# A pipelined cross-attention: the maximum of a slot spread over the partitions by DMA instead of TensorE and ScalarE

## The chip, the cores and the metric

The program runs on one core of one Trainium2 chip. The metric is the device time of one execution in microseconds (us): lower is better. An execution is timed from launch to end; the profile of one execution shows the engines of that core from their first to their last instruction. Engine names: PE is TensorE (PEld its weight loads), DVE is VectorE, ACT is ScalarE, POOL is GpSimd, SP is SyncE, which here only issues DMAs.

## What is computed

The reference is one layer of a perceiver: cross-attention of 8 batches of 128 latents to 2048 context rows each, then differential self-attention, then a mixture of 8 experts, each added to the input. Only the cross-attention is touched here:

```python
q = (query @ wq.T + bq)   # 8 batches x 128 rows, 16 heads of 32
k = (key @ wk.T + bk)     # 8 batches x 2048 rows
v = (value @ wv.T + bv)
scores = einsum('bhqd,bhkd->bhqk', q, k) / sqrt(32)
attn = softmax(scores, axis=-1)
ctx = einsum('bhqk,bhkd->bhqd', attn, v)
return ctx @ wo.T + bo
```

## The kernel before

Five stages follow each other: queries and the first context chunk (names with a_), the cross-attention (b_), its output projection (c_), the projections of the self-attention (d_), and the self-attention with the experts (e_ and f_). The change lies in the second, the function cross_attention.

A slot is one batch and one group of four heads (HG = 4), so there are 32 slots (SLOTS). A slot takes four chunks (CHUNK) of 512 context rows. Scores are computed with context rows on the partitions and the 4 x 128 queries of four heads along the free axis. A softmax over context rows then runs partly across partitions. For the maximum the kernel first reduces elementwise over all 16 blocks of a slot, into b_mx (128 partitions x 4 heads x 128 queries). TensorE transposes b_mx into a bank (the unit "M"), DVE reduces each row to one number per query and head (b_top, 128 x 4), and now queries lie on partitions. These 512 numbers have to come back as one row that all 128 partitions hold (b_mb, 128 x 512), since the subtraction `b_s - b_mb` (L892) has context rows on the partitions again. Before the change this way back is: ACT copies b_top 128 times wide into b_spread (L849), TensorE transposes b_spread (the unit "B", four transposes at L765), ACT copies the bank into b_mb (L837).

All engines follow one clock of "beats", eight to a slot, written out by hand: at each beat every engine's program runs the steps whose rule names that beat. The functions `score_step`, `exp_step`, `turned_slot` and so on hold the rules. For slot m, counted from its own beats:

- beat 8m+27: TensorE runs M(m). Beat 8m+28: DVE reduces it to b_top, and before, ACT spreads it and TensorE ends the beat with B(m). Beat 8m+29: ACT moves B(m) to b_mb.
- even beats: TensorE computes the scores of one chunk into the four banks b_psS (L720, 16 matmuls); DVE takes them into b_mx in four steps (L926, L929); in the next, odd beat ACT moves all of b_psS to one of seven buffers b_s (L871), and only then may TensorE write the next chunk's scores there.
- even beats, five chunks behind the scores: DVE subtracts the maximum (L892), ACT takes the exponential (L854), POOL adds the four blocks up for the denominators (L650 for a slot's first chunk, twice L655 for each other one). The first chunk of slot m has its turn at beat 8m+30.
- beats 2 mod 4: TensorE multiplies two chunks of exponentials with the values (L734). Beat 8m+40: it sums the denominators (L757), DVE takes the reciprocal and normalizes (L914, L918), ACT adds a bias (L861).
- every beat up to 255: TensorE projects one unit of keys or values, 12 matmuls of 128x512 (L43 to L45), into one of three banks b_work, which M and B share too; ACT takes each away in the next beat (L809, L821 or L830). DVE transposes a block of the context (L882), ACT rounds it (L846), POOL takes the rest (L639), SP loads the block after next (L222, four DMAs).

TAIL is 28: the last four slots sum their denominators on TensorE (L748) in place of POOL. From beat 256 on nothing is projected any more. Within an engine everything runs in the order of its program; between engines semaphores order it.

Of the kernel before, what the change touches and what calls it, by code (L numbers as in the profile page):

```python
# [7 lines left out]
F32 = mybir.dt.float32  # L8
F32R = mybir.dt.float32r
BF16 = mybir.dt.bfloat16  # L10
ALU = mybir.AluOpType
# [4 lines left out]
P = 128  # L16
# [432 lines left out]
def cross_attention(nc, x, ctx_in, w, q_d, o_d, cin, kT, shared):  # L449

    with ExitStack() as ctx:
# [74 lines left out]
        for beat in range(FIRST, LAST):  # L526
            if (x0 := projected(beat)) is not None:
                p0, u0 = x0
                enter(("KV"[u0 // CHUNK], p0, u0 % CHUNK), beat)
            if (s0 := turned_slot(beat)) is not None:  # L530
                enter(("M", s0, 0), beat)
            if (s0 := spread_slot(beat)) is not None:
                enter(("B", s0, 0), beat)

        def value_places(b, t):
# [22 lines left out]
        psO = ctx.enter_context(nc.psum_tensor("b_psO", [P, 512], F32))  # L558

        const = sem("b_const")  # L560
        turned = sem("b_turned")
        bias_in = sem("b_bias_in")
        q_in = [sem(f"b_q_in{i}") for i in range(3)]
# [20 lines left out]
        def _(sp):  # L584
# [12 lines left out]
            sp.wait_ge(turned, 1)  # L597
            load_blocks(sp, ctx_in, cin, shared.raw_in, 2, 2)
            for beat in range(FIRST, LAST):
                if (x0 := turned_next(beat - 1)) is not None and x0[0] * CHUNK + x0[1] + 2 < SLOTS * CHUNK:  # L600
                    u = x0[0] * CHUNK + x0[1]
                    sp.wait_ge(turned, u - 2 * CHUNK + 1)
                    load_blocks(sp, ctx_in, cin, shared.raw_in, *divmod(u + 2, CHUNK))
                n = score_step(beat - 1)
                if n is not None and n % CHUNK == CHUNK - 1 and n // CHUNK + 3 < SLOTS:

                    sp.wait_ge(s_full, n + 1)
                    load_queries(n // CHUNK + 3)
                n = normal_slot(beat - 1)
                if n is not None and n < SLOTS - 1:  # L610
                    b, g = divmod(n, G)
                    sp.wait_ge(o_done, n + 1)
                    sp.dma_start(o_d[g, b, :, :], o_st[:, n % 2, :]).then_inc(o_out[n % 2], 16)
                if beat == SLOTS * SLOT + 2:

                    sp.wait_ge(work_full, RING["V", SLOTS - 1, CHUNK - 1] + 1)
                    sp.dma_start(shared.wo, w["wo"].rearrange("(o p) d -> p o d", p=P)).then_inc(shared.wo_in, 16)
                    sp.dma_start(shared.x1, x.rearrange("b p d -> p b d")).then_inc(shared.x_in, 16)
                if n == SLOTS - 3:

                    for i in range(2):
                        sp.wait_ge(o_out[i], 16 * G * (B - 1) // 2)
                    for g in range(G):
                        sp.dma_start(shared.o_sb[:, g, 0:B - 1, :], o_d[g, 0:B - 1].rearrange("b p t -> p b t")
                                     ).then_inc(shared.o_in[0], 16)
                if n == SLOTS - 2:
                    for i in range(2):
                        sp.wait_ge(o_out[i], 16 * (SLOTS // 2 - i))
                    for g in range(G - 1):
                        sp.dma_start(shared.o_sb[:, g, B - 1, :], o_d[g, B - 1]).then_inc(shared.o_in[1], 16)  # L630
# [39 lines left out]
        def _(pe):  # L670
            pe.wait_ge(const, 1)

            def wait_evicted(unit):
                if unit is not None:
                    kind, m, n = unit
                    if kind == "K":
                        pe.wait_ge(k_done, m * CHUNK + n + 1)
                    elif kind == "V":
                        pe.wait_ge(v_done, m * CHUNK + n + 1)
                    elif kind == "M":  # L680
                        pe.wait_ge(top_done, m + 1)
                    else:
                        pe.wait_ge(mb_done, m + 1)

            def bank_of(unit):
                wait_evicted(LAST_IN[unit])
# [81 lines left out]
            for beat in range(FIRST, LAST):  # L768
# [11 lines left out]
                        values(p, u - CHUNK)  # L780
                if (m := turned_slot(beat)) is not None:
                    turn("M", m, mx, mx_done, (m + 1) * MAXIMA)
                if (m := spread_slot(beat)) is not None:
                    turn("B", m, spread, spread_done, m + 1)
                    if m == SLOTS - 1:

                        pe.wait_ge(shared.wo_in, 16)
# [1 line left out]
                        for k in range(KD):  # L789
# [2 lines left out]
                                                           shared.wo[:, o, k * P:(k + 1) * P], ident[:, :])  # L792
                            last.then_inc(shared.wo_full, 1)

        @block.scalar
        def _(act):
            act.wait_ge(bias_in, 32)
            for beat in range(FIRST, LAST):
                if beat > FIRST and (x0 := projected(beat - 1)) is not None:
# [11 lines left out]
                    else:  # L811
# [11 lines left out]
                        else:  # L823
# [4 lines left out]
                            else:  # L828
                                out = rows[:, :, at[0]:at[0] + P]
                            nc.scalar.activation(out, bank[:, :].rearrange("p (g r) -> p g r", g=G),  # L830
                                                 ACT.Copy).then_inc(v_done, 1)
                if (m := spread_slot(beat - 1)) is not None:
                    i, bank = RING["B", m, 0], work[BANK["B", m, 0]]
                    act.wait_ge(work_full, i + 1)

# [6 lines left out]
                if (x0 := transposed(beat)) is not None:  # L842
# [1 line left out]

                    act.wait_ge(turned, (p - 2) * CHUNK + k + 1)
                    nc.scalar.activation(cT[0][:, p % 2, k, :], cin[:, 1, k % 2, :], ACT.Copy).then_inc(hi_done, 1)  # L846
                if (m := spread_slot(beat)) is not None:
                    act.wait_ge(top_done, m + 1)
                    nc.scalar.activation(spread[:, :, :], top[:, m % 2, :].rearrange("p (j o) -> p j o", o=1)  # L849
                                         .broadcast_to([P, HG, P]), ACT.Copy).then_inc(spread_done, 1)  # L850
                if (n := exp_step(beat)) is not None:
                    act.wait_ge(sub_done, n + 1)
                    part = s[:, n % BUFS, :, :].rearrange("p t n -> p (t n)")
                    nc.scalar.activation(part, part, ACT.Exp, scale=SCALE).then_inc(exp_done, 1)  # L854
                if (m := normal_slot(beat)) is not None:
                    g = m % G
                    act.wait_ge(od_free, m + 1)
# [5 lines left out]
                if (n := move_step(beat)) is not None:  # L863

                    act.wait_ge(mx_done, CHUNK * (n + 1))
                    if n >= BUFS:

                        act.wait_ge(pv_done, n - BUFS + 1)
                        if (n - BUFS) // CHUNK < TAIL:
                            act.wait_ge(sum_done, sums_of(n - BUFS))  # L870
                    nc.scalar.activation(s[:, n % BUFS, :, :].rearrange("p t (j q) -> p t j q", j=HG),  # L871
                                         psS[:, :, :].rearrange("p j (t q) -> p t j q", t=CHUNK),
                                         ACT.Copy).then_inc(s_moved, 1)

        @block.vector
        def _(dve):
            def context_turned(p, k):

                u = (p - 2) * CHUNK + k
# [4 lines left out]
            dve.wait_ge(bias_in, 32)  # L884
            context_turned(2, 0)
            for beat in range(FIRST, LAST):
                if (n := exp_step(beat)) is not None:
                    m, c = divmod(n, CHUNK)
                    dve.wait_ge(s_moved, n + 1)
                    if c == 0:  # L890
                        dve.wait_ge(mb_done, m + 1)
                    nc.vector.tensor_tensor(  # L892
                        s[:, n % BUFS, :, :], s[:, n % BUFS, :, :],
                        mb[:, :].rearrange("p (o n) -> p o n", o=1).broadcast_to([P, CHUNK, HG * P]),
                        ALU.subtract).then_inc(sub_done, 1)
                if (m := spread_slot(beat)) is not None:
                    i, bank = RING["M", m, 0], work[BANK["M", m, 0]]
                    dve.wait_ge(work_full, i + 1)

                    reached(dve, spread_done, m - 1)  # L900
                    nc.vector.tensor_reduce(top[:, m % 2, :], bank[:, :].rearrange("p (j k) -> p j k", j=HG),
                                            AX.X, ALU.max).then_inc(top_done, 1)
                if (m := normal_slot(beat)) is not None:
# [17 lines left out]
                if (n := score_step(beat)) is not None:  # L921
                    dve.wait_ge(s_full, n + 1)
                    for t in range(CHUNK):
# [3 lines left out]
                        else:  # L927
                            dve.wait_ge(mx_done, n * CHUNK + t)
                            nc.vector.tensor_tensor(mx[:, :, :], part, mx[:, :, :], ALU.max).then_inc(mx_done, 1)  # L929


def transpose_units(nc, pe, bank, ident, src, blocks, u, full, lo_done):
# [1038 lines left out]
```

## Time and profile before

| | us |
|---|---|
| median of 3 runs | 1692.62 |
| lowest and highest of them | 1683.69 and 1693.33 |
| the profiled execution | 1690.8 |
| its span, first to last instruction | 1689.0 |

The mean granted clock of TensorE in the profiled execution is 0.973 of full speed. The span is 1.8 us shorter than the execution's own time. The cross-attention lies between about 71 and 1130 us of the span.

### The profile page before, as it was taken

To read this page: it belongs to the slowest core of one execution; us is meant where nothing else is said; L and a number is where in the kernel's file an instruction comes from. 1 tells how busy PE (TensorE), PEld (TensorE's weight loads), DVE (VectorE), ACT (ScalarE), POOL (GpSimd) and SP (SyncE) were. 2 spreads that over 40 slices of the span, in tenths; PEclk is the share of its full clock that TensorE was granted. 3 is DMA by queue.
4 is the path that set the end of the run, shared out by engine and by line. 5 is a ranking of instruction groups with operands and counts; after the bars stand their busy time and mean duration, and the time that the engine had idled before them with its cause. 6 is when DMAs were issued, how large, how long until landed. Compare 5 with 4: busy or idle time off the path is not lost. (4 is left out here: it accounts for less than half of the span.)

```text
span 1689.0 us, 36984 instructions
## 1 busy us (share of the span) xinstructions
PE 1619.8 (96%) x15589; PEld 1314.5 (78%) x15604; DVE 1179.0 (70%) x1523; ACT 950.8 (56%) x1437; POOL 899.7 (53%) x472
## 2 busy tenths in 40 slices
PE   7999999999999999999999999667998899999999
PEld 6788888888888888888888887556886677777787
DVE  5137888888888888888888887877434577653322
ACT  4347776777767777777777776662103677630000
POOL 0026788888878878888887885002000344522220
PEclk9999999999999999999999999788999799899999
DMA  5332222222222222222222210213422111211001
GB/s 187 75 50 35 36 39 40 39 38 37 38 37 42 36 36 40 41 36 37 37 40 37 40 24 5 80 53 113 165 88 94 38 51 51 65 50 50 28 23 50
DMA packets 310404, 88.75 MB, mean 53 GB/s; under 512 B 259392, under 2 KB 292160, under 8 KB 310240
## 3 DMA queue, kind: packets, MB, share of 16 engines
q1 hardware_dynamic: 310240, 86.39, 22.2%
q8 instruction: 124, 2.03, 0.5%
q14 instruction: 40, 0.33, 0.1%
HBM read 71.67 MB, written 14.68 MB: 51 GB/s over the span
## 5 line engine op out<-in xcount | busy, mean ns | idle before, releaser
L655 POOL TENSOR_TENSOR b_acc<-b_acc,b_s 128x1024 f32<-128x1024 f32 x168 | 563.6, 3355 | 12.4 <-ACT b_s L854 5.3
L892 DVE TENSOR_TENSOR b_s<-b_s,b_mb 128x2048 f32<-128x2048 f32 x128 | 398.0, 3111 | 28.4 <-ACT b_mb L837 28.4
L929 DVE TENSOR_TENSOR b_mx<-b_psS,b_mx 128x512 f32<-128x512 f32 x480 | 330.8, 689 | 93.3 <-PE b_psS L720 80.2
L854 ACT ACTIVATE b_s<-b_s 128x2048 f32<-128x2048 f32 x128 | 244.3, 1909 | 18.3 <-DVE b_s L892 15.2
L871 ACT ACTIVATE b_s<-b_psS 128x2048 f32<-128x2048 f32 x128 | 241.2, 1885 | 20.9 <-DVE b_mx L929 20.9
L43 PE MATMUL b_work<-wvT,cT 128*128 128x512 f32 x496 | 202.9, 409 | 0.0
L43 PE MATMUL b_work<-cT,wkT 128*128 128x512 f32 x496 | 200.3, 404 | 1.7 <-POOL b_ones L636 1.7
L44 PE MATMUL b_work<-wvT,cT 128*128 128x512 f32 x496 | 194.5, 392 | 0.0
L44 PE MATMUL b_work<-cT,wkT 128*128 128x512 f32 x496 | 194.2, 392 | 0.0
L45 PE MATMUL b_work<-wvT,cT 128*128 128x512 f32 x496 | 193.8, 391 | 0.0
L45 PE MATMUL b_work<-cT,wkT 128*128 128x512 f32 x496 | 193.4, 390 | 0.0
L639 POOL TENSOR_TENSOR cT<-cin,cT 128x512 fp32r<-128x512 f32 x120 | 156.1, 1301 | 54.8 <-ACT cT L846 54.8
L720 PE MATMUL b_psS<-b_q,b_kT 32*128 32x128 f32 x4096 | 153.8, 287 | 12.9 <-ACT b_s L871 12.8
L809 ACT ACTIVATE b_kT<-b_work,b_bk 128x512 f32<-128x512 f32 x124 | 85.5, 689 | 140.5 <-PE b_work L45 140.5
L720 PEld LDWEIGHTS b_psS<-b_q,b_kT 32*128 32x128 f32 x4096 | 129.3, 190 | 38.7 <-issue 38.7
L650 POOL TENSOR_TENSOR b_acc<-b_s 128x1024 f32<-128x1024 f32 x28 | 68.8, 2456 | 129.7 <-PE b_psO L757 127.8
L734 PE MATMUL b_psO<-b_s,v_sb 128*32 128x128 f32 x4096 | 129.7, 278 | 2.5 <-issue 1.8
L734 PEld LDWEIGHTS b_psO<-b_s,v_sb 128*32 128x32 f32 x4096 | 110.3, 111 | 24.8 <-issue 24.4
L43 PEld LDWEIGHTS b_work<-cT,wkT 128*128 128x128 f32 x496 | 93.0, 187 | 27.5 <-POOL b_ones L636 2.1
L882 DVE STREAM_TRANSPOSE cin<-cin 128x512 f32<-128x512 f32 x120 | 83.8, 699 | 41.7 <-DMA b_bv<-in_L_xattn_bv 19.5
L43 PEld LDWEIGHTS b_work<-wvT,cT 128*128 128x128 f32 x496 | 93.1, 188 | 24.6
L1707 ACT ACTIVATE e_sm<-e_psS,e_low 128x128 f32<-128x128 f32 x256 | 90.1, 383 | 37.7 <-DVE e_low L1782 37.7
(290 smaller groups left out, 2802.4 us busy)
## 6 DMA issues: line engine op xcount, KB each, us to landing
cin<-in_ctx SPq DMA_DIRECT2D x480, 64.0 KB, 2.4
experts_sb<-in_L_ffn_expert_w SPq DMA_DIRECT2D x8, 1024.0 KB, 5.3
q_scratch<-d_st SPq DMA_DIRECT2D x16, 256.0 KB, 2.3
k_scratch<-d_st SPq DMA_DIRECT2D x16, 256.0 KB, 2.3
e_q<-q_scratch SPq DMA_DIRECT2D x16, 256.0 KB, 2.7
k_sb<-k_scratch SPq DMA_DIRECT2D x16, 256.0 KB, 2.9
cin<-in_ctx SPq DMA_DIRECT2D x4, 512.0 KB, 8.4
b_kT<-in_x SPq DMA_DIRECT2D x4, 512.0 KB, 8.0
```

The lines of the kernel that those rows point to most:

```text
L43: nc.tensor.matmul(out, lhs[0], rhs[0], start=first, stop=False)
L44: nc.tensor.matmul(out, lhs[0], rhs[1], start=False, stop=False)
L45: return nc.tensor.matmul(out, lhs[1], rhs[0], start=False, stop=last)
L639: nc.gpsimd.tensor_tensor(cT[1][:, p % 2, k, :], cin[:, 1, k % 2, :], f32(cT[0][:, p % 2, k, :]), ALU.subtract).then_inc(split_done, 1)
L655: nc.gpsimd.tensor_tensor(acc[:, :, :], acc[:, :, :], s[:, buf, 2 * i:2 * i + 2, :], ALU.add).then_inc(sum_done, 1)
L720: last = nc.tensor.matmul(psS[:, j, t * P:(t + 1) * P], kT[h, at + t * P:at + (t + 1) * P], q[h, m % 3, :], start=True, stop=True)
L734: last = nc.tensor.matmul(psO[j * HD:(j + 1) * HD, 0:P], v[:, at + j * HD:at + (j + 1) * HD], s[:, n % BUFS, i, j * P:(j + 1) * P], start= ...
L854: nc.scalar.activation(part, part, ACT.Exp, scale=SCALE).then_inc(exp_done, 1)
L871: nc.scalar.activation(s[:, n % BUFS, :, :].rearrange("p t (j q) -> p t j q", j=HG), psS[:, :, :].rearrange("p j (t q) -> p t j q", t=CHUN ...
L892: nc.vector.tensor_tensor(s[:, n % BUFS, :, :], s[:, n % BUFS, :, :], mb[:, :].rearrange("p (o n) -> p o n", o=1).broadcast_to([P, CHUNK, ...
L929: nc.vector.tensor_tensor(mx[:, :, :], part, mx[:, :, :], ALU.max).then_inc(mx_done, 1)
L1707: last = nc.scalar.activation(sm[:, hf, i, j % 2, u, :], psS[:, j, u, :], ACT.Exp, bias=low[:, hf, j, u:u + 1], scale=-1.0, accum_out=sums ...
```

## The change

For slots 0 to 27 the way back from b_top to b_mb goes through DRAM. SP waits for b_top, stores its 512 numbers to a scratch tensor (one element of four bytes each, so that four rows of 128 queries lie one behind the other), waits until they have landed, and loads that row of 2 KB into all 128 partitions of b_mb. This stands in SP's program at beat 8m+29, ahead of the loads of the context block. The unit B, ACT's spread and ACT's move are gone for these slots; slots 28 to 31 keep them.

For the same slots the first chunk's subtraction moves on DVE from the start of its beat (8m+30) to the end, behind the maxima of that beat, and ACT's exponential of it from beat 8m+30 to the end of beat 8m+31, behind that beat's move of b_psS. The other three chunks of a slot keep their places.

```diff
-            if (s0 := spread_slot(beat)) is not None:
+            if (s0 := spread_slot(beat)) is not None and s0 >= TAIL:
                 enter(("B", s0, 0), beat)
...
+        top_d = nc.dram_tensor("top_scratch", [TAIL, HG, P], F32).ap()
+        top_out = [sem(f"b_top_out{i}") for i in range(2)]
+        mb_in = sem("b_mb_in")
...
             for beat in range(FIRST, LAST):
+                if (m := spread_slot(beat - 1)) is not None and m < TAIL:
+                    sp.wait_ge(top_done, m + 1)
+                    with nc.allow_non_contiguous_dma(reason="512 numbers"):
+                        sp.dma_start(top_d[m].rearrange("j p -> p j"), top[:, m % 2, :]).then_inc(top_out[m % 2], 16)
+                    sp.wait_ge(top_out[m % 2], 16 * (m // 2 + 1))
+
+                    reached(sp, sub_done, m * CHUNK)
+                    sp.dma_start(mb[:, :], top_d[m].rearrange("(o j) p -> o (j p)", o=1).broadcast_to([P, HG * P])
+                                 ).then_inc(mb_in, 16)
...
-                if (m := spread_slot(beat)) is not None:
-                    turn("B", m, spread, spread_done, m + 1)
+                if (m := spread_slot(beat)) is not None and m >= TAIL:
+                    turn("B", m, spread, spread_done, m - TAIL + 1)
...
+        def late(n):
+
+            return n % CHUNK == 0 and n // CHUNK < TAIL
...
-                if (m := spread_slot(beat - 1)) is not None:
+                if (m := spread_slot(beat - 1)) is not None and m >= TAIL:
...
-                if (m := spread_slot(beat)) is not None:
+                if (m := spread_slot(beat)) is not None and m >= TAIL:
                     act.wait_ge(top_done, m + 1)
...
-                if (n := exp_step(beat)) is not None:
-                    act.wait_ge(sub_done, n + 1)
...
+                if (n := exp_step(beat)) is not None and not late(n):
+                    exponentials(n)
...
+                if (n := exp_step(beat - 1)) is not None and late(n):
+                    exponentials(n)
...
+            def less_maximum(n):
+                m, c = divmod(n, CHUNK)
+                dve.wait_ge(s_moved, n + 1)
+                if c == 0 and m < TAIL:
+                    dve.wait_ge(mb_in, 16 * (m + 1))
+                elif c == 0:
+                    dve.wait_ge(mb_done, m - TAIL + 1)
...
-                if (n := exp_step(beat)) is not None:
-                    m, c = divmod(n, CHUNK)
...
+                if (n := exp_step(beat)) is not None and not late(n):
+                    less_maximum(n)
...
-                    reached(dve, spread_done, m - 1)
+                    if m >= TAIL + 2:
+                        dve.wait_ge(spread_done, m - TAIL - 1)
+                    elif m >= 2:
+                        dve.wait_ge(top_out[m % 2], 16 * (m // 2))
...
+                if (n := exp_step(beat)) is not None and late(n):
+                    less_maximum(n)
```

On PE, at the seam between the value units of beats 8m+28 and 8m+29, the program before reads:

```order
L43 MATMUL b_work<-wvT_69,cT_52 128x512
L44 MATMUL b_work<-wvT_70,cT_52 128x512
L45 MATMUL b_work<-wvT_69,cT_53 128x512
L765 MATMUL b_work<-ident,b_spread 128x128 x4
L43 MATMUL b_work<-wvT_69,cT_52 128x512
L44 MATMUL b_work<-wvT_70,cT_52 128x512
```

The four transposes of b_spread stand between two units of the projection; in the changed program the units follow each other there, and nothing else on PE moves.

On DVE, from the subtraction of a slot's last chunk to that of the next slot's second one, the program before (L892 is the subtraction, L901 the reduction to b_top, L882 the context's transpose, L926 and L929 the maxima, L914 and L918 the normalization):

```order
L892 TENSOR_TENSOR b_s<-b_s,b_mb 128x2048
L901 TENSOR_REDUCE b_top<-b_work 128x4
L882 STREAM_TRANSPOSE cin<-cin 128x512
L926 COPY b_mx<-b_psS 128x512
L929 TENSOR_TENSOR b_mx<-b_psS,b_mx 128x512 x3
L892 TENSOR_TENSOR b_s<-b_s,b_mb 128x2048
L882 STREAM_TRANSPOSE cin<-cin 128x512
L929 TENSOR_TENSOR b_mx<-b_psS,b_mx 128x512 x4
L892 TENSOR_TENSOR b_s<-b_s,b_mb 128x2048
L914 RECIPROCAL b_rD<-b_psO 128x128
L918 TENSOR_TENSOR b_oq<-b_psO,b_rD 128x128
```

And the changed program at the same place (L906 is the subtraction, L931 the reduction, L916 the transpose, L956 and L959 the maxima):

```order
L906 TENSOR_TENSOR b_s<-b_s,b_mb 128x2048
L931 TENSOR_REDUCE b_top<-b_work 128x4
L916 STREAM_TRANSPOSE cin<-cin 128x512
L956 COPY b_mx<-b_psS 128x512
L959 TENSOR_TENSOR b_mx<-b_psS,b_mx 128x512 x3
L916 STREAM_TRANSPOSE cin<-cin 128x512
L959 TENSOR_TENSOR b_mx<-b_psS,b_mx 128x512 x4
L906 TENSOR_TENSOR b_s<-b_s,b_mb 128x2048 x2
L944 RECIPROCAL b_rD<-b_psO 128x128
L948 TENSOR_TENSOR b_oq<-b_psO,b_rD 128x128
```

The first chunk's subtraction went past one transpose and one set of maxima, so that it stands directly ahead of the second chunk's.

## Rows read from the trace of the kernel before

**Rows 1.** The page, part 1: busy time and share of the engines.

```profile
PE 1619.8 (96%) x15589; PEld 1314.5 (78%) x15604; DVE 1179.0 (70%) x1523; ACT 950.8 (56%) x1437; POOL 899.7 (53%) x472
```

**Rows 2.** The view by stretches: one slot; PE, PEld, DVE, ACT, POOL busy, clock, DMA.

```profile
615.00:647.40 32.40, 32.40 (x377) 26.26 (x376) 27.86 (x28) 23.27 (x23) 27.47 (x12) 1.00 0.23 38
```

**Rows 3.** The waits of PE, whole run: total us, times, longest.

```profile
PE b_psS L720 <- ACT b_s L871: 12.8, 6, 5.0
...
PE b_work L765 <- DVE b_mx L929: 9.2, 3, 3.1
```

**Rows 4.** Timeline of PE in that slot: start, us, line, operation, out<-in.

```profile
619.24 0.39 PE L45 MATMUL b_work<-wvT,cT 128*128 128x512 f32 x1
619.47 0.60 PE L765 MATMUL b_work<-ident,b_spread 128*128 128x128 f32 x4
619.83 0.48 PE L43 MATMUL b_work<-wvT,cT 128*128 128x512 f32 x1
620.14 0.39 PE L44 MATMUL b_work<-wvT,cT 128*128 128x512 f32 x1
...
624.64 1.17 PE L720 MATMUL b_psS<-b_q,b_kT 32*128 32x128 f32 x32
...
631.45 0.64 PE L757 MATMUL b_psO<-b_acc,b_ones 128*32 128x128 f32 x16
...
638.79 1.96 PE L734 MATMUL b_psO<-b_s,v_sb 128*32 128x128 f32 x64
640.67 1.17 PE L720 MATMUL b_psS<-b_q,b_kT 32*128 32x128 f32 x32
```

**Rows 5.** Timeline of DVE: the first slot's second subtraction, then that slot.

```profile
142.89 2.28 DVE L892 TENSOR_TENSOR b_s<-b_s,b_mb 128x2048 f32<-128x2048 f32 x1
...
615.97 0.68 DVE L901 TENSOR_REDUCE b_top<-b_work 128x4 f32<-128x512 f32 x1
...
620.86 3.21 DVE L892 TENSOR_TENSOR b_s<-b_s,b_mb 128x2048 f32<-128x2048 f32 x1 [0.84 <-ACT b_mb L837]
...
625.88 2.87 DVE L929 TENSOR_TENSOR b_mx<-b_psS,b_mx 128x512 f32<-128x512 f32 x4 [1.19 <-PE b_psS L720]
628.66 2.28 DVE L892 TENSOR_TENSOR b_s<-b_s,b_mb 128x2048 f32<-128x2048 f32 x1
632.16 0.96 DVE L914 RECIPROCAL b_rD<-b_psO 128x128 f32<-128x128 f32 x1 [1.22 <-PE b_psO L757]
...
633.98 2.83 DVE L929 TENSOR_TENSOR b_mx<-b_psS,b_mx 128x512 f32<-128x512 f32 x4
636.73 3.70 DVE L892 TENSOR_TENSOR b_s<-b_s,b_mb 128x2048 f32<-128x2048 f32 x1
```

**Rows 6.** Timeline of ACT in that slot.

```profile
631.55 0.60 ACT L830 ACTIVATE v_sb<-b_work 128x512 f32<-128x512 f32 x1 [0.34 <-PE b_work L45]
632.05 0.62 ACT L846 ACTIVATE cT<-cin 128x512 fp32r<-128x512 f32 x1
632.57 1.91 ACT L854 ACTIVATE b_s<-b_s 128x2048 f32<-128x2048 f32 x1
...
636.85 1.89 ACT L871 ACTIVATE b_s<-b_psS 128x2048 f32<-128x2048 f32 x1
```

**Rows 7.** Timeline of POOL: its first accumulation, then that slot.

```profile
143.40 4.02 POOL L650 TENSOR_TENSOR b_acc<-b_s 128x1024 f32<-128x1024 f32 x1 [1.94 <-ACT b_s L854]
...
619.51 6.81 POOL L655 TENSOR_TENSOR b_acc<-b_acc,b_s 128x1024 f32<-128x1024 f32 x2
626.27 1.30 POOL L639 TENSOR_TENSOR cT<-cin,cT 128x512 fp32r<-128x512 f32 x1
632.27 2.39 POOL L650 TENSOR_TENSOR b_acc<-b_s 128x1024 f32<-128x1024 f32 x1 [4.70 <-PE b_psO L757]
```

**Rows 8.** POOL's L655 alone: durations of one, ns, least/median/most.

```profile
L655 POOL TENSOR_TENSOR b_acc<-b_acc,b_s x168: 2393/2435/4341, 148.7 to 1043.5; 128x1024 f32<-128x1024 f32 x168
```

**Rows 9.** DMA issues by tensor: KB each, median us from issue to landing.

```profile
cin<-in_ctx SPq DMA_DIRECT2D x480, 64.0 KB, 2.4
...
c_bo<-in_L_xattn_bo SPq DMA_DIRECT2D x1, 256.0 KB, 3.2
...
b_bk<-in_L_xattn_bk SPq DMA_DIRECT2D x1, 2.0 KB, 2.5
```

More of the change, by code:

```diff
@@ L682, in wait_evicted @@
                     else:
-                        pe.wait_ge(mb_done, m + 1)
+                        pe.wait_ge(mb_done, m - TAIL + 1)
             def bank_of(unit):
@@ L793, in _, with exponentials @@
                             last.then_inc(shared.wo_full, 1)
+        def late(n):
+            return n % CHUNK == 0 and n // CHUNK < TAIL
         @block.scalar
         def _(act):
+            def exponentials(n):
+                act.wait_ge(sub_done, n + 1)
+                part = s[:, n % BUFS, :, :].rearrange("p t n -> p (t n)")
+                nc.scalar.activation(part, part, ACT.Exp, scale=SCALE).then_inc(exp_done, 1)
             act.wait_ge(bias_in, 32)
@@ L850, in _ @@
                                          .broadcast_to([P, HG, P]), ACT.Copy).then_inc(spread_done, 1)
-                if (n := exp_step(beat)) is not None:
-                    act.wait_ge(sub_done, n + 1)
-                    part = s[:, n % BUFS, :, :].rearrange("p t n -> p (t n)")
-                    nc.scalar.activation(part, part, ACT.Exp, scale=SCALE).then_inc(exp_done, 1)
+                if (n := exp_step(beat)) is not None and not late(n):
+                    exponentials(n)
                 if (m := normal_slot(beat)) is not None:
@@ L873, in _ @@
                                          ACT.Copy).then_inc(s_moved, 1)
+                if (n := exp_step(beat - 1)) is not None and late(n):
+                    exponentials(n)
         @block.vector
         def _(dve):
+            def less_maximum(n):
[5 more added lines that the diff above has]
+                    dve.wait_ge(mb_done, m - TAIL + 1)
+                nc.vector.tensor_tensor(
+                    s[:, n % BUFS, :, :], s[:, n % BUFS, :, :],
+                    mb[:, :].rearrange("p (o n) -> p o n", o=1).broadcast_to([P, CHUNK, HG * P]),
+                    ALU.subtract).then_inc(sub_done, 1)
             def context_turned(p, k):
@@ L886, in _ @@
             for beat in range(FIRST, LAST):
-                if (n := exp_step(beat)) is not None:
-                    m, c = divmod(n, CHUNK)
[L889 to L895, printed above, removed]
+                if (n := exp_step(beat)) is not None and not late(n):
+                    less_maximum(n)
                 if (m := spread_slot(beat)) is not None:
```

## The prediction

> **What bounds the kernel now.** I read the busy shares first: PE is at 96% of the span, DVE at 70%, the others lower [rows 1]. That is an average, so the second view is the one by stretches, cut to one slot of the cross-attention: in 32.40 us PE is busy for 32.40, at a granted clock of 1.00, the upper of its two levels (2.4 GHz); DVE is busy 27.86, POOL 27.47, ACT 23.27 [rows 2]. PE has no gap at all there, so a slot is worth what PE's instructions take, and only what leaves PE's queue can shorten it. The third view, PE's waits over the whole run, says the same from the other side: the waits in this stage are few, 12.8 us in 6 for the scores' banks and 9.2 us in 3 for the maxima [rows 3]. They lie almost wholly in the last four slots, where nothing is projected any more and which the change leaves alone. The fourth view is the timeline of the engines in that same slot, where I look for what PE comes close to waiting for. I keep the trace's own times below and move PE's marks behind B by what B's removal gives.
>
> **What is removed.** Per slot four transposes leave PE. Their busy time of 0.60 us overlaps their neighbours, so I go by starts. The last matmul of one unit starts at 619.24 and the transposes at 619.47, a step of 0.23. The next unit starts at 619.83, and its second matmul at 620.14 [rows 4]. Without the transposes the next unit would start at 619.47 and its second matmul 0.23 later, at 619.70. The gain is 620.14 - 619.70 = 0.44 us a slot, and 28 x 0.44 = 12.3 us in all. The bounds of this term from the same rows: 0.36 (619.83 - 619.47, if the slow first step comes back elsewhere) gives 10.1, the full 0.60 gives 16.8. I take 0.44 because it counts to where the steady step has returned.
>
> ACT loses its spread and its move to b_mb, both off the path: it was idle 9 us of the slot [rows 2], so they are worth nothing. DVE's wait of 0.84 us for b_mb [rows 5] goes too, and buys nothing either, since DVE next waits 1.19 us for the scores.
>
> **What is added, first the two DMAs.** The trace has no store of 512 single numbers. The nearest rows: the load of a bias of 512 numbers with the same strides, landed 2.5 us after its issue, and the context loads, landed after 2.4. The load of one 2 KB row into 128 partitions exists, as c_bo: 3.2 us [rows 9]. b_top is ready at 615.97 + 0.68 = 616.65 [rows 5], so b_mb is ready at about 616.65 + 2.5 + 3.2 = 622.4. The subtraction that needs it comes at 628.2 (below): 5.8 us to spare. The lower bound of the chain is 2.4 + 2.4, the upper one I set by letting the store take three times its row: 7.5 + 3.2, at 627.4, still in time. So the term is 0 at either end. SP's queue: the block's four loads stand behind the pair and go out about 6 us later. They land in 2.4 us and are used two transposes later, some 16 us on, so this is hidden too. DMA engines were busy 0.23 of the slot [rows 2].
>
> The Trainium skill, "DMA: Bandwidth & Descriptors", Specifications, speaks against this store: below 512 bytes a descriptor is a read-modify-write. It gives no price for 512 of them. The trace here shows loads of such pieces only; no row shows the store, and by the margin above the rule would have to cost more than 5 us to matter.
>
> **What is moved, and what comes close.** The first chunk's subtraction now follows the maxima of its beat. In the new schedule PE's marks behind B are 0.44 earlier: the scores at 624.20, the denominators at 631.01, the values' product at 638.35, the next scores but one at 640.23 [rows 4]. That last one must find b_psS moved by ACT. This is the wait I check.
>
> How long a subtraction takes depends on POOL. It took 2.28 at 628.66, while POOL stood idle between 627.57 and 632.27, but 3.21 at 620.86 and 3.70 at 636.73 with POOL at work [rows 5, 7]. The pair of L655 beside the one at 620.86 took 6.81, where one alone takes about 2.4 [rows 7, 8]: 619.51 + 2.4 = 621.9, then the subtraction until 624.07, then the second accumulation until 626.3. And the first L650 of the kernel, started at 143.40 inside the subtraction of 142.89 to 145.17, took 4.02 in place of 2.4, ending 2.3 us after it. One simply waits for the other. The Trainium skill, "SBUF — State Buffer", Who interferes with whom, states this as an exclusive lock held for a whole instruction; by that rule, the trace agrees. Had I gone by the rows' mere durations instead, the moved subtraction would keep 3.21 and the margin below would be nearly gone.
>
> Now DVE, step by step. Maxima of the beat: start 625.88 - 0.44 = 625.44, end 2.78 later (628.66 - 625.88), 628.22. POOL's accumulations of the slot before ended at 626.27 with one subtraction inside; that subtraction has moved away, so POOL is through earlier, about 625, and its rest step L639 too. It is idle then, because L650 needs the exponential. So: first subtraction 628.22 to 630.50, second to 632.78, both at 2.28. Then reciprocal, normalization and transpose, 633.98 - 632.16 = 1.82, to 634.60 (the denominators are there since 631.7). Then the next maxima, 636.73 - 633.98 = 2.75, to 637.35, which is 0.62 later than before. ACT's move follows, 1.89, to 639.3 [rows 6]. PE wants to start the scores at 640.23: 0.9 us to spare, no wait.
>
> ACT: the move of the beat's scores ends at about 630.8 (628.22, a take-away of 0.6, 1.9), the late exponential at 632.7, take-away and rounding 0.60 + 0.62, the second exponential at 635.8 [rows 6]. The product of values needs it at 638.35: 2.5 to spare. POOL starts L650 at 632.7 in place of 632.27 and has the earlier 2.3 us in hand. DVE's fourth subtraction ends at about the time it did, so M and the reduction stay in place.
>
> **The sum.** 12.3 us gained on PE, nothing given back. From the profiled execution: 1690.8 - 12.3 = 1678.5. That execution lies 1.8 below the median of the three runs shown, which run from 1683.69 to 1693.33.
>
> **Rivals.**
> - *Late maxima (slower).* The place is the scores at 640.23 behind ACT's move. It decides once DVE is more than 0.9 us later than I have it. This would be so if the two subtractions don't get 2.28 each. For it: they now stand back to back, DVE works through what it had spread out, and two more durations exist in the rows. Against it: POOL has nothing to do just then. At 3.21 each the delay is 1.86, the wait 1.0 with a signal between engines, the net loss 1.0 - 0.44 = 0.5 to 0.6 a slot: +16, 1707. At 3.70 each the delay is 2.84, the net loss about 1.5: +42, 1733. The trace of the first is nearer.
> - *No gain.* Half of that delay, 1.3 us a slot, costs just the 0.44: 1690.8. Or the step over the seam comes back at another instruction. For it: another queue (the scores' banks) is within 0.9 us of PE. Against: PE waited there for nothing in the slot.
> - *The DMA chain is late.* It decides above 11.6 us (628.22 - 616.65) for store and load, twice the rows' sum. At 14 us the first subtraction would be 2.4 late, the wait on PE 1.5, the net 1.1 a slot: +30, 1721. No row speaks for a landing that long at a DMA share of 0.23.
> - *It doesn't do what it says.* PE's program has 5252 rows against 5280, so 28 units are gone, one a slot. I give this nothing.
>
> **How the numbers follow.** Forecast 0.74, late maxima 0.12, no gain 0.10, late DMA 0.04. About 1% is what a measurement of this kernel can tell from no change (the three runs spread over 0.6%). The forecast is a gain of 0.73% and falls within it; the spread of the runs and the upper bound of the PE term (16.8) put 0.14 beyond 1%. Late maxima at 1707 is still just within 1%, the heavier form and the late DMA are not: 0.09 slower. The rest, 0.77, is the same. The range takes the PE term's bounds (1674 to 1680.7), 3 us for the runs' spread below, and reaches up past the case of no gain: 1671 to 1694. What is left out is the late maxima and the late DMA, 0.16.
>
> **What would show it.** Right: a slot of 31.96 us with PE busy throughout; B's transposes 16 in place of 128; the first and second subtraction about 2.28 each, back to back; the first not preceded by a wait for a DMA; ACT's move ending about 0.9 us ahead of the scores; the store landing in about 2.5 us and b_mb in 3.2. Wrong: rows of PE at the scores waiting for ACT's b_s inside slots 0 to 27, subtractions of 3 us or more there, or DVE waiting for b_mb<-top_scratch.

## The result, and the profile after

The change makes the kernel slower: 1739.26 us (median of 4 runs, 1729.22 to 1744.48) against 1688.15 for the kernel before, a ratio of 1.030 with a 95% interval of 1.023 to 1.036. The profiled execution took 1744.48, with a span of 1742.7. Executions of one and the same kernel here fall on two levels some 8 us apart (before: 1683.7 and 1692.6), and the difference lies in the stages behind the cross-attention, so I compare stretches inside the stage where I can.

The busy shares, to be laid beside [rows 1]:

```profile
PE 1627.5 (93%) x15477; PEld 1319.1 (76%) x15492; DVE 1115.6 (64%) x1523; ACT 912.6 (52%) x1381; POOL 850.4 (49%) x472
```

PE lost its 112 transposes (15589 to 15477 instructions) and is nevertheless busy for longer, 1627.5 us against 1619.8, while its share falls. The first suggests that it ran at a lower clock somewhere, the second that it waits. PE's waits in the run after, against [rows 3] (12.8 in 6 there):

```profile
PE b_psS L733 <- ACT b_s L891: 48.5, 31, 5.0
...
PE b_psS L733 <- issue: 8.6, 8, 3.9
```

So 25 more waits at the scores for ACT's move, nearly one a slot, and eight in which PE waited for nothing that the profile names. Now one slot, in order. SP's timeline with the two new DMAs:

```profile
371.07 0.39 SPq L607 DMA_DIRECT2D top_scratch<-b_top  x1
379.91 0.33 SPq L611 DMA_DIRECT2D b_mb<-top_scratch  x1
```

DVE in the same slot (its counterpart is [rows 5]):

```profile
370.35 0.69 DVE L931 TENSOR_REDUCE b_top<-b_work 128x4 f32<-128x512 f32 x1 [0.24 <-PE b_work L778]
...
385.42 4.49 DVE L906 TENSOR_TENSOR b_s<-b_s,b_mb 128x2048 f32<-128x2048 f32 x2 [2.42 <-DMA b_mb<-top_scratch]
389.83 0.95 DVE L944 RECIPROCAL b_rD<-b_psO 128x128 f32<-128x128 f32 x1
...
391.65 2.83 DVE L959 TENSOR_TENSOR b_mx<-b_psS,b_mx 128x512 f32<-128x512 f32 x4
```

And what PE meets at the scores, between two M units:

```profile
369.71 0.60 PE L778 MATMUL b_work<-ident,b_mx 128*128 128x128 f32 x4
...
396.54 1.17 PE L733 MATMUL b_psS<-b_q,b_kT 32*128 32x128 f32 x32 [1.54 <-ACT b_s L891]
...
403.22 0.60 PE L778 MATMUL b_work<-ident,b_mx 128*128 128x128 f32 x4
```

b_top is ready at 371.04 and SP issues the store at once, but can issue the load only at 379.91: the store takes 8.8 us, where I had put 2.5. The subtraction starts 5.5 after the load's issue, once the load has landed: DVE, idle for 2.42 until then, starts it 14.4 us after b_top. The pair of subtractions takes 4.49, as forecast. All that follows is late by the rest: maxima, ACT's move, and PE's scores by 1.54. The slot takes 403.22 - 369.71 = 33.51 us against 32.40 before [rows 2].

In the issue list the load has a median landing of 5.3 us, where c_bo had 3.2 [rows 9]:

```profile
b_mb<-top_scratch SPq DMA_DIRECT2D x28, 256.0 KB, 5.3
```

The distance from store to load on SP is 8.7 to 9.5 us in 20 of the 28 slots, and 9.7 to 11.4 in the others, seven of which stand in a row. In that row lies the worst of the "issue" waits. PE's timeline there:

```profile
622.49 0.73 PE L733 MATMUL b_psS<-b_q,b_kT 32*128 32x128 f32 x16
627.15 1.28 PE L733 MATMUL b_psS<-b_q,b_kT 32*128 32x128 f32 x16 [3.94 <-issue]
...
629.38 0.63 PE L45 MATMUL b_work<-wvT,cT 128*128 128x512 f32 x1
629.80 0.63 PE L43 MATMUL b_work<-wvT,cT 128*128 128x512 f32 x1
```

PE stops in the midst of one set of scores, whose data are all there, while the store of 615.60 is in flight (the load goes out at 627.01). PE goes on 0.14 us later. The end of the pause and the end of the store fall together in the other slots too: seven of the eight "issue" waits end within 0.6 us of the issue of the load, 8.8 to 11.6 us after the store's own. Afterwards PE's matmuls step by 0.42 to 0.43 us in place of 0.23 [rows 4]. The view by stretches (columns as in [rows 2]) shows the granted clock around it:

```profile
615.00:622.00 7.00, 7.00 (x77) 5.76 (x80) 4.46 (x7) 5.40 (x5) 6.92 (x4) 1.00 0.07 3
622.00:627.00 5.00, 1.22 (x38) 1.10 (x29) 0.00 (x0) 0.00 (x0) 2.55 (x2) 0.84 0.00 0
627.00:633.00 6.00, 5.85 (x28) 4.67 (x28) 4.43 (x5) 0.00 (x0) 0.00 (x0) 0.56 0.63 124
```

After the idle 4 us the clock is at its lower level of 1.2 GHz for some 5 us (0.56 of full over the third stretch, whose last piece has PE back at a step of 0.23). The DMA engines' share is 0.00 from 622 to 627, though the store isn't through.

### The profile page after: what moved, and what is told of

Read it like the earlier page. It is cut to its first block and busy times, and to the rows that moved or that the text cites. A ratio compares the mean times of both kernels' runs of the same rounds, so it can differ in the third digit from the quotient of the medians.

```text
span 1742.7 us, 36732 instructions
## 1 busy us (share of the span) xinstructions
PE 1627.5 (93%) x15477; PEld 1319.1 (76%) x15492; DVE 1115.6 (64%) x1523; ACT 912.6 (52%) x1381; POOL 850.4 (49%) x472
## 3 DMA queue, kind: packets, MB, share of 16 engines
q8 instruction: 123, 2.02, 0.6%
## 5 line engine op out<-in xcount | busy, mean ns | idle before, releaser
L668 POOL TENSOR_TENSOR b_acc<-b_acc,b_s 128x1024 f32<-128x1024 f32 x168 | 515.3, 3067 | 7.8 <-ACT b_s L817 0.9
L959 DVE TENSOR_TENSOR b_mx<-b_psS,b_mx 128x512 f32<-128x512 f32 x480 | 329.8, 687 | 155.1 <-PE b_psS L733 142.0
L906 DVE TENSOR_TENSOR b_s<-b_s,b_mb 128x2048 f32<-128x2048 f32 x128 | 333.0, 2621 | 61.7 <-DMA b_mb<-top_scratch 55.0
L733 PE MATMUL b_psS<-b_q,b_kT 32*128 32x128 f32 x4096 | 163.7, 292 | 57.3 <-ACT b_s L891 48.5
L733 PEld LDWEIGHTS b_psS<-b_q,b_kT 32*128 32x128 f32 x4096 | 136.9, 193 | 86.1 <-issue 85.8
L916 DVE STREAM_TRANSPOSE cin<-cin 128x512 f32<-128x512 f32 x120 | 84.3, 703 | 80.1 <-POOL cT L652 54.9
L852 ACT ACTIVATE v_sb<-b_work 128x512 f32<-128x512 f32 x80 | 47.5, 594 | 146.4 <-PE b_work L45 146.4
```

The source lines that it names most:

```text
L668: nc.gpsimd.tensor_tensor(acc[:, :, :], acc[:, :, :], s[:, buf, 2 * i:2 * i + 2, :], ALU.add).then_inc(sum_done, 1)
L733: last = nc.tensor.matmul(psS[:, j, t * P:(t + 1) * P], kT[h, at + t * P:at + (t + 1) * P], q[h, m % 3, :], start=True, stop=True)
L906: nc.vector.tensor_tensor(s[:, n % BUFS, :, :], s[:, n % BUFS, :, :], mb[:, :].rearrange("p (o n) -> p o n", o=1).broadcast_to([P, CHUNK, ...
```

## The experiments

Three theories stood at the start. Theory 1: b_mb comes too late, the rest is as forecast. Theory 2: the transfers disturb PE and its clock, whatever they bring. Theory 3: the late order of subtraction and exponential costs by itself. Softmax doesn't change when the same number is subtracted for one query and head throughout, so runs that subtract something else do the same work. Each run's diff is shown against the changed kernel where nothing else is said, and only its telling lines.

**No DMA of the maximum**

```diff
-                if (m := spread_slot(beat - 1)) is not None and m < TAIL:
-                    sp.wait_ge(top_done, m + 1)
...
+            nc.gpsimd.memset(mb[:, :], 1.0).then_inc(const, 1)
```

> The changed kernel without both DMAs: b_mb is set once to 1.0 by POOL, so that for slots 0 to 27 a constant is subtracted in place of the maximum; the order stays late, the unit B stays away. Theory 1 (the maximum comes too late, and everything else is as forecast): b_mb is always there, so PE gains its 0.44 us a slot and waits for nothing: 12 us less than before, about 1676 against 1688. Theory 2 (the two transfers disturb PE and its clock, whatever they bring): the same 1676. Theory 3 (the late order itself squeezes DVE and ACT so that PE waits at the scores): still about 1730 to 1740, with PE waiting 1 to 2 us a slot for ACT's move.

Measured: 1679.13, ratio 0.9926 (0.991 to 0.9943). Two M units of it, and DVE between them:

```profile
607.87 0.60 PE L770 MATMUL b_work<-ident,b_mx 128*128 128x128 f32 x4
...
639.82 0.60 PE L770 MATMUL b_work<-ident,b_mx 128*128 128x128 f32 x4
```

```profile
621.09 4.48 DVE L898 TENSOR_TENSOR b_s<-b_s,b_mb 128x2048 f32<-128x2048 f32 x2
```

The slot takes 31.95 us; 31.96 was forecast. The gain on PE and the back-to-back subtractions at 2.28 each are there. Theory 3 falls.

**The load alone**

```diff
-                        sp.dma_start(top_d[m].rearrange("j p -> p j"), top[:, m % 2, :]).then_inc(top_out[m % 2], 16)
-                    sp.wait_ge(top_out[m % 2], 16 * (m // 2 + 1))
...
-                    sp.dma_start(mb[:, :], top_d[m].rearrange("(o j) p -> o (j p)", o=1).broadcast_to([P, HG * P])
+                    sp.dma_start(mb[:, :], w["bk"].rearrange("(o n) -> o n", o=1).broadcast_to([P, HG * P])
```

> The changed kernel with the load but without the store: SP waits for b_top and loads 512 numbers of a bias into all partitions of b_mb, so a bias is subtracted in place of the maximum. Theory 1: the load alone lands 3 to 6 us after b_top, before the 11.6 us at which it is wanted: about 1676. Theory 2, if the load of 256 KB is what disturbs: 1690 to 1720, with waits of PE put down to issue. Theory 3: 1730 to 1740.

Measured: 1678.99, ratio 0.9922 (0.9905 to 0.9938). The load lands in 3.3 us and costs nothing. What is wrong lies in the store.

**The late order alone, in the kernel before** (the diff is against that kernel)

```diff
-                if (n := exp_step(beat)) is not None:
+                if (n := exp_step(beat)) is not None and not late(n):
...
+                if (n := exp_step(beat)) is not None and late(n):
+                    less_maximum(n)
```

> The kernel before with the late order alone: first chunk's subtraction and exponential moved as in the change, the unit B and ACT's copies kept, no DMA of the maximum. Theories 1 and 2: no difference from before beyond 0.3%, about 1688, PE 100% busy in a slot. Theory 3: slower by 40 us or more.

Measured: 1692.63, ratio 1.0009 (0.9994 to 1.0024), PE busy for 850.00 us of the 850 from 200 to 1050. The order is free.

**The store aside, and nobody waits**

```diff
+                    sp.dma_start(mb[:, :], w["bk"].rearrange("(o n) -> o n", o=1).broadcast_to([P, HG * P])
+                                 ).then_inc(mb_in, 16)
                         sp.dma_start(top_d[m].rearrange("j p -> p j"), top[:, m % 2, :]).then_inc(top_out[m % 2], 16)
-                    sp.wait_ge(top_out[m % 2], 16 * (m // 2 + 1))
```

> The same load from the bias, and behind it the store of b_top as in the changed kernel, for which nobody waits but the reduction two slots later; a bias is subtracted in place of the maximum. The store runs, but nothing hangs on it. Theory 1: about 1676, the store costs nothing. Theory 2: the store of 512 single numbers itself disturbs (instruction fetch of PE, context loads behind it): 1690 to 1720, with waits of PE put down to issue and a lower clock behind them. Theory 3: 1730 to 1740.

Measured: 1712.42, ratio 1.0117 (1.0086 to 1.0147), 33 us above the load alone. PE's waits:

```profile
PE b_psS L731 <- ACT b_s L889: 16.9, 14, 5.0
PE b_psS L731 <- issue: 15.9, 13, 2.6
```

b_mb is in time here, and few waits for ACT's move are added (16.9 us against 12.8 before); the waits put down to "issue" are the largest new group. From 200 to 1050 us there are 15 of them, and each ends 9.0 to 11.5 us after a store was issued. The store disturbs by itself, as theory 2 has it, in this form: four context loads stand right behind it in the queue.

**The same, but SP waits for the store before it goes on** (the diff is against the run above)

```diff
                         sp.dma_start(top_d[m].rearrange("j p -> p j"), top[:, m % 2, :]).then_inc(top_out[m % 2], 16)
+                    sp.wait_ge(top_out[m % 2], 16 * (m // 2 + 1))
```

> As the run with the store aside (b_mb from a bias, loaded first), but SP waits for the store before it goes on, so that its duration can be read; store and destination as in the change, 512 pieces of four bytes, neighbours next to each other in DRAM. A bias is subtracted in place of the maximum. The store takes 9 us or more between its issue and the next block load; the kernel is at 1700 to 1715 as with the store aside (1712), if the store's disturbance has to do with the store alone; at 1679, if it was the context loads queued behind it that disturbed.

Measured: 1681.65, ratio 0.9919 (0.9887 to 0.9952). From the store's issue to the next load it is 7.3 to 9.5 us. PE's waits for "issue" are down to:

```profile
PE b_psS L732 <- issue: 2.0, 4, 0.6
```

One wait of SP makes 31 us. The store alone in flight costs some 3 us by the medians (1681.65 against 1678.99, within the spread of its four runs, 1671.17 to 1686.41); it is costly with other loads queued behind it. These four waits too end within 0.4 us of the next load's issue, which is when SP has seen the store through. In the changed kernel SP waits as well, yet its profiled execution has eight of the "issue" waits. So this disturbance isn't tied to the loads queued behind alone.

**As late, without a store.** The first try:

```diff
+                    for i in range(5):
+                        sp.dma_start(spread[0:1, 0, :], w["bk"][0:P].rearrange("(o n) -> o n", o=1)).then_inc(idle_in, 16)
+                        sp.wait_ge(idle_in, 16 * (5 * m + i + 1))
```

> The changed kernel without the store, but as late: in its place SP loads 128 numbers of a bias five times, each waited for (about 2.1 us each), and then the bias into b_mb, so b_mb lands some 14 us after b_top as in the changed kernel; a bias is subtracted in place of the maximum. Theory 1 (lateness alone costs a wait of 1 to 2 us at the scores a slot, on top of what the store disturbs): 1700 to 1715 and PE's waits at the scores for ACT's move in nearly every slot. Theory 2 (it is all the store's disturbance): 1679.

Measured: 1678.96, ratio 0.9933 (0.9911 to 0.9954). It doesn't put theory 1 to the test: five loads took 6 us, so b_mb was there 9.7 us after b_top. It does bear out that 9.7 is early enough. With nine of them:

> As the run with five small loads in place of the store, but with nine, since five took only 6 us together and b_mb landed 9.7 us after b_top, still in time. Nine take about 10.9 us, and with the load's 3.6 b_mb lands 14.5 us after b_top, as in the changed kernel (9.0 + 5.3), 2.9 after the 11.6 at which DVE wants it. A bias is subtracted in place of the maximum. Theory 1 (lateness costs by itself): DVE waits 2 to 3 us for b_mb in each slot, PE 1 to 2 us at the scores for ACT's move, 1700 to 1720. Theory 2 (only the store's disturbance costs): 1679.

Measured: 1723.56 (four runs, 1715.83 to 1731.08), ratio 1.0172 (1.0148 to 1.0197), 45 us above the run with five. Waits of PE, and the slot's rows on DVE and PE:

```profile
PE b_psS L733 <- ACT b_s L891: 55.1, 33, 5.0
```

```profile
607.07 0.69 DVE L929 TENSOR_REDUCE b_top<-b_work 128x4 f32<-128x512 f32 x1 [1.89 <-PE b_work L778]
...
622.25 4.50 DVE L906 TENSOR_TENSOR b_s<-b_s,b_mb 128x2048 f32<-128x2048 f32 x2 [2.52 <-ACT b_s L891]
```

```profile
606.43 0.60 PE L778 MATMUL b_work<-ident,b_mx 128*128 128x128 f32 x4
...
633.36 1.17 PE L733 MATMUL b_psS<-b_q,b_kT 32*128 32x128 f32 x32 [1.64 <-ACT b_s L891]
...
640.09 0.60 PE L778 MATMUL b_work<-ident,b_mx 128*128 128x128 f32 x4
```

The subtraction starts 2.5 us after the maxima ended. The view puts this down to ACT, whose move of a later chunk ended just then, at 622.19; but the chunk subtracted here was moved five chunks earlier, and the load was issued at 618.74, with a median landing of 3.4 us in this run. It is the load. PE waits 1.64, the slot takes 33.66. Over the whole run PE's waits for ACT's move are 42 us more than in the kernel before (55.1 against 12.8 [rows 3]), and it has none of the "issue" waits at the scores. Without any store, lateness gives about three quarters of what separates the changed kernel from the load alone (45 of 1739.26 - 1678.99 = 60).

**What makes the store slow.** Four forms. First, 16 bytes a partition, heads innermost:

```diff
-                        sp.dma_start(top_d[m].rearrange("j p -> p j"), top[:, m % 2, :]).then_inc(top_out[m % 2], 16)
+                    sp.dma_start(top_d[m], top[:, m % 2, :]).then_inc(top_out[m % 2], 16)
...
+                    less = mb[:, :].rearrange("p (o q j) -> p o j q", o=1, j=HG).broadcast_to([P, CHUNK, HG, P])
```

> The changed kernel with the store as 128 pieces of 16 bytes (b_top as it lies, queries outermost) in place of 512 of four; the row loaded back then has the four heads innermost, and the subtraction reads b_mb with a step of four elements. Everything is computed. Theory A (the store's time and its disturbance go by the number of pieces; 9 us for 512, some 2 us of it fixed): SP's time from store to load falls to about 4 us, PE has no more waits put down to issue, and the kernel lands near the one with the load alone, 1679 to 1685. Theory B (any store of pieces this small is slow, however many): the time stays at 9 us and the kernel at 1730 to 1740. A strided read that is slower on DVE would show in the subtraction (2.28 now).

Measured: 1803.07, ratio 1.0667 (1.0625 to 1.071). The store lands in 1.4 us at the median (1.4 to 3.4 to the load's issue), and the transport is no longer a problem. The store's issue row, and the subtraction:

```profile
top_scratch<-b_top SPq DMA_DIRECT2D x28, 2.0 KB, 1.4
```

```profile
L906 DVE TENSOR_TENSOR b_s<-b_s,b_mb x128: 2281/2293/4531, 148.3 to 1185.8; 128x2048 f32<-128x2048 f32 x128
```

```profile
L911 DVE TENSOR_TENSOR b_s<-b_s,b_mb x128: 2281/4004/5866, 144.0 to 1251.4; 128x2048 f32<-128x2048 f32 x128
```

The second fence is the changed kernel's, the third this run's (least, median and most of one, ns): read with a step of four elements, a subtraction takes 4.00 us in place of 2.29. DVE's longer steps reach PE: DVE is busy for 752 of the 850 us from 200 to 1050, PE waits 72.5 us in 29 for ACT's move, and ACT's move 63.5 us in 48 for DVE's maxima. The kernel loses 124 us against the load alone.

Second, the 512 numbers each in a row of 512 bytes of its own, with b_mb from the bias, loaded first, and a wait for the store, as in the waited store aside:

```diff
-        top_d = nc.dram_tensor("top_scratch", [TAIL, HG, P], F32).ap()
+        top_d = nc.dram_tensor("top_scratch", [TAIL, HG, P, P], F32).ap()
...
+                        sp.dma_start(top_d[m].rearrange("j p w -> p j w")[:, :, 0], top[:, m % 2, :]).then_inc(top_out[m % 2], 16)
```

> The same with the 512 pieces of four bytes written 512 bytes apart, so that no two share a line of DRAM. If the price comes from many engines writing into the same lines, the store falls to 2 or 3 us and the kernel to 1679; if it comes from the number of pieces, store and kernel stay as with the waited store aside (9 us, 1700 to 1715).

Measured: 1678.41, ratio 0.9905 (0.988 to 0.993); the store takes 3.0 to 4.0 us. Third, in the same order, one head's 128 numbers, side by side:

```diff
+                        sp.dma_start(top_d[m].rearrange("j p -> p j")[:, 0:1], top[:, m % 2, 0:1]).then_inc(top_out[m % 2], 16)
```

> The same as the waited store aside, but only one head's 128 numbers are stored, 128 pieces of four bytes, neighbours next to each other; three heads' maxima are left out. If the price goes by the number of pieces, the store takes 1.4 us, as the 128 pieces of 16 bytes did, or up to 3.5, and the kernel is at 1679 to 1683. If it goes by neighbours in one line (128 numbers in 512 bytes, as each head has in the change), it takes clearly longer than 1.4 us, though fewer are written.

Measured: 1671.68, ratio 0.9883 (0.9867 to 0.990). The issue lists of the two runs, the 512 apart first:

```profile
top_scratch<-b_top SPq DMA_DIRECT2D x28, 2.0 KB, 3.1
```

```profile
top_scratch<-b_top SPq DMA_DIRECT2D x28, 0.5 KB, 7.2
```

A quarter of the pieces side by side takes 7.2 us, all of them apart 3.1. So the price isn't their number. It is that pieces of four bytes from different partitions fall next to each other in DRAM. Pieces of 16 bytes side by side don't pay it; whether the size of a piece or the distance from one start to the next decides was not separated, since no run stored four bytes at a distance between 4 and 512. The Trainium skill, "DMA: Bandwidth & Descriptors", Specifications, says that the DMA engines do read-modify-write on transfers below 512 bytes. The runs fit this in part. That one such write has to wait for its neighbour's would explain the slow ones, but no run shows it; and the 16-byte pieces and the four-byte pieces set apart are below 512 bytes too, and landed in 1.4 and 3.1 us. So being below 512 bytes isn't what makes the 9 us here.

Fourth, a form that computes everything: one DVE transpose puts each head's numbers for 32 queries in one row.

```diff
+                        nc.vector.transpose(topT[:, m % 2, :], top[:, m % 2, :]).then_inc(topT_done, 1)
...
+                    for i in range(4):
+                        sp.dma_start(top_d[m][:, 32 * i:32 * i + 32], topT[32 * i:32 * i + HG, m % 2, :]
+                                     ).then_inc(top_out[m % 2], 16)
```

> The changed kernel with b_top turned by one more DVE transpose of 128x32, so that the 512 numbers lie in 16 rows of 128 bytes, stored by four DMAs of four rows each; everything is computed. Theory A: store to load about 3.5 us (four issues of 0.4 and a landing of 2.2), no waits of PE put down to issue, 1678 to 1684. Theory B: still slow, 1730 or so.

Measured: 1672.44 (6 runs), ratio 0.9898 (0.9869 to 0.9927): 1.0% under the kernel before, and clearly faster than the changed one. In the stage itself, from 100 us to the transposes of w_o, its profiled execution takes 1010.9 us against 1021.9 before: 11.0 gained, near the 12.3 of PE's term. The rest of the distance between the medians lies behind the stage. Rows of SP, ACT and PE:

```profile
610.77 1.28 SPq L610 DMA_DIRECT2D top_scratch<-b_topT  x4
612.92 0.34 SPq L615 DMA_DIRECT2D b_mb<-top_scratch  x1
```

```profile
631.46 1.88 ACT L896 ACTIVATE b_s<-b_psS 128x2048 f32<-128x2048 f32 x1 [0.88 <-DVE b_mx L969]
```

```profile
609.16 0.60 PE L783 MATMUL b_work<-ident,b_mx 128*128 128x128 f32 x4
...
634.38 1.17 PE L738 MATMUL b_psS<-b_q,b_kT 32*128 32x128 f32 x32
...
641.11 0.60 PE L783 MATMUL b_work<-ident,b_mx 128*128 128x128 f32 x4
```

From the first of the four stores to the load it is 2.15 us, the slot is 31.95, and ACT's move ends at 633.3, 1.0 us ahead of the scores (0.9 was forecast).

**That form in the order of before**

```diff
-            return n % CHUNK == 0 and n // CHUNK < TAIL
+            return False
```

> The run with b_top turned and stored in 16 rows of 128 bytes, but with the first chunk's subtraction and exponential back at their places of before (at the start of beat 8m+30, ahead of that beat's maxima). Everything is computed. With the short transport b_mb is there about 6.5 us after b_top; the order of before asks for it 4.2 us after it (620.86 against 616.65), so DVE waits 2.2 us, and then POOL's accumulation stands beside the subtraction again. If the moved order is needed: the maxima of that beat end 1 to 2 us later than before, still before PE wants the scores two beats on, so 1672 to 1690, with a small loss against the late order. If it isn't needed at all: the same as the late order within 0.3% (1672 to 1679).

Measured: 1686.67, ratio 0.9964 (0.995 to 0.9978). DVE meets the wait where it was expected (2.2 us; the load was issued at 616.51, and the move of ACT that the row names ended at 619.76 and is a later chunk's):

```profile
619.82 4.15 DVE L911 TENSOR_TENSOR b_s<-b_s,b_mb 128x2048 f32<-128x2048 f32 x1 [2.14 <-ACT b_s L896]
```

By the spans of the two profiled executions the early order costs 6.0 us (1684.6 against 1678.6): PE's waits for ACT's move are 16.7 us in 18 in place of 13.5 in 5, which is some 3 of the 6; what the others are stays open. So the moved order, free by itself, makes room for even the short transport.

## Why the prediction was wrong

- **The gain on PE, 0.44 us a slot, 12.3 in all: right.** The runs without DMA and with the load alone gained 13.0 and 13.2 us (against 1692.14); the slot shown of the first takes 31.95.
- **The moved order, costing nothing: right.** 1.0009 alone. Both subtractions took 2.28 back to back, since POOL stood idle, and the margin at the scores was 1.0 for 0.9.
- **The load, 3.2 us: right alone** (3.3), but 5.3 behind the store in the changed kernel and 4.5 behind the 16-byte pieces. With the 16 rows of 128 bytes it was 3.3 again.
- **"The trace has no store of 512 single numbers. The nearest rows: the load of a bias": the step that failed.** I took 2.5 us, and set the upper bound by three times that, 7.5. It took 8.7 to 11.4, and with the load behind it the chain in the slot shown came to 14.4 us, where I had 5.7. Both ends came from loads, where the pieces are read side by side; the runs show that what costs is writing four-byte pieces side by side. The prediction's sentence on what the Trainium skill, "DMA: Bandwidth & Descriptors", Specifications, says of read-modify-write stood there, and I gave it no price because no row had one. That no row spoke for a long landing wasn't evidence against it: no row spoke on it at all.
- **The rival of the late DMA chain was the one that came, at a chance of 0.04.** Its place was right, and its turning point, 11.6 us, lies where the runs have it: 9.7 us cost nothing, and 14.5 in the run of nine loads cost 45. By its own working a start 14.4 us after b_top is 2.8 late, leaves PE a wait of 2.8 - 0.9 = 1.9 and a net loss of 1.9 - 0.44 = 1.5 a slot, 41 us. The slot shown has a wait of 1.54 and a net loss of 1.1; its maxima ended 12.0 us after b_top in place of 11.6, and the margin at the scores was 1.0 for 0.9 where the store was quick, which accounts for the most of it; the run of nine loads has a wait of 1.64 and is 32 us above the kernel before.
- **What the rival hadn't in it:** the pauses of PE put down to "issue", and the lower clock behind them. From 100 us to the transposes of w_o, PE is idle for 70.9 us of 1075.3 in the changed kernel, 25.1 of 1008.5 in the run without DMA, and busy for 1004.4 against 983.4. The stretch is 66.8 us longer: 45.8 of it are idle time, and 21.0 are the same instructions taking longer. The granted clock, read in stretches of 1 us and weighted with PE's busy time, accounts for 24.1 us in the changed kernel and 10.7 without DMA, so for some 13 of the 21.0; what the other 8 are stays open. Nor does the lower clock need a store: by the same reckoning the run of nine loads lost 19.2.
- **SP's later context loads: hidden, as said,** in the runs where SP waits (9.8 us later with the waited store, with some 3 us lost). With the loads queued behind a store in flight they weren't, and this case I hadn't seen.

Left open: why PE pauses while such a store is in flight. The pauses end when the store does, but a slow store alone doesn't bring them: the run that stores one head's numbers, in 7.2 us, has none at the scores. The page of the profile lists a queue of the kind "instruction" (123 packets, 2.02 MB), so PE's own instructions may come by DMA and be held up by the store; no view shows these transfers, so this is only inferred. Also open is why the load behind it lands in 5.3.

## What to carry to other kernels

A transfer for which the trace has no row of the same direction and the same shape has no price, and its upper bound must not be made from rows of another kind; where a margin hangs on it, time that one DMA first. Numbers that lie a few to a partition are better turned on chip before they are stored, as this case shows it: 16 rows of 128 bytes took 2.15 us from first store to load, and 512 single numbers side by side 9. A layout chosen to ease a DMA has to be read by an engine afterwards: a step of four elements cost DVE 1.7 us on each of the subtractions and the kernel 124 us against the load alone, more than the 60 of the slow store.

## What the runs showed of the hardware that was not expected

Stores to DRAM from 128 partitions, issued from SP: 512 pieces of four bytes side by side 7.3 to 9.5 us to SP's next issue (8.7 to 11.4 in the changed kernel), 128 such pieces 7.2 at the median, 512 of them 512 bytes apart 3.1, 128 pieces of 16 bytes side by side 1.4. A load of 512 bytes to one partition, waited for and repeated, took 1.2 us a time. While the slow store is in flight PE can stop for up to 3.9 us with its data at hand, and go on when the store is through; with four context loads queued behind the store this made 13 waits at the scores and a kernel 33 us slower than with the load alone. A wait for b_mb was put down to ACT in two of the rows above, where the move of ACT that DVE needed had long been through.
